# Shared experts of a mixture-of-experts layer on one core: from token-stationary tiles with transposes to weight-stationary chunks over two tiles

## The reference

```python
xn = _layernorm(x)
s  = attention(xn)                 # 16 query heads of 128, 4 key/value heads, rotary, causal
def ffn(x):                        # x: 2048 x 256
    scores = softmax(x @ gate_w.T) # 16 experts, the best 2 per token
    y  = sum over the token's 2 experts e of weight_e * (silu(x @ Wg_e) * (x @ Wu_e)) @ Wd_e    # 176 hidden
    gu = x @ shared_gate_up        # 256 x 704: gate 352 columns, up 352 columns
    y += (silu(gu[:, :352]) * gu[:, 352:]) @ shared_down                                       # 352 x 256
out = x + s * silu(ffn(xn))
```

## Time and profile before

| what | us |
|---|---|
| median of 3 runs | 671.38 |
| the profiled execution, whole | 671.35 |
| its span (first to last instruction) | 669.5 |
| busy: PE, DVE, ACT, POOL | 641.6, 538.2, 469.5, 482.7 |

### The profile page before, as it was taken

How to read it: one execution, slowest core, us unless ns; L and a number is a source line. 1 busy time by engine, 2 the same in 40 slices (tenths; PEclk the granted TensorE clock), 3 DMA queues, 4 the chain that set the end, 5 groups by cost and what they waited for, 6 DMA issues and landing times.

```text
span 669.5 us, 15670 instructions
## 1 busy us (share of the span) xinstructions
PE 641.6 (96%) x5108; PEld 462.9 (69%) x5171; DVE 538.2 (80%) x1621; ACT 469.5 (70%) x1271; POOL 482.7 (72%) x563
## 2 busy tenths in 40 slices
PE   7889999999999999999999999999999999999994
PEld 6656777767677677767677676767776777777772
DVE  4999999999999999999999999999974553333356
ACT  5799897868676676766686766767697745555542
POOL 4898979776667676788777878677769945555545
PEclk9999999999999999999999999999999999999998
DMA  8980001112500000000010101000144716667764
GB/s 287 347 260 1 2 9 25 24 11 41 155 1 1 1 1 2 1 33 27 25 40 8 40 8 40 25 17 1 51 68 139 196 26 145 139 143 137 223 248 164
DMA packets 70832, 52.11 MB, mean 78 GB/s; under 512 B 41392, under 2 KB 64144, under 8 KB 70768
## 3 DMA queue, kind: packets, MB, share of 16 engines
q1 hardware_dynamic: 66432, 40.57, 23.2%
q0 software_dynamic: 3792, 10.43, 5.1%
q10 hardware_dynamic: 544, 0.28, 0.2%
HBM read 24.75 MB, written 18.77 MB: 65 GB/s over the span
## 4 chain that ended last, share of the span: by engine, by line
PE 71%; DVE 12%; ACT 8%; issue 5%; DMA 2%; POOL 1%; SPq 0%; DVEq 0%; ACTq 0%
PE bank L1654 12%; PE bank L1592 12%; PE bank L1671 10%; PE bank L1623 9%; PE bank L1801 9%; PE bank L1638 8%; PE bank L1835 6%; PE bank L1810 2%; PE bank L1607 2%; DVE arena L1318 2%; ACT arena L956 2%; DVE arena L1291 2%; DVE arena L1290 1%; ACT arena L970 1%; ACT arena L964 1%
## 5 line engine op out<-in xcount | busy, mean ns | idle before, releaser
L956 ACT ACTIVATE arena<-bank,nmax 128x448 f32<-128x448 f32 (+7 forms) x256 | 125.8, 507 | 34.6 <-DVE nmax L1306 34.2
L655 POOL TENSOR_TENSOR arena<-arena,rinv 128x64 f32<-128x64 f32 (+2 forms) x192 | 102.2, 561 | 64.4 <-DVE rinv L1312 64.1
L970 ACT CAST arena<-bank 128x512 f16<-128x512 f32 (+1 forms) x192 | 94.5, 524 | 41.9 <-PE bank L1638 41.0
L1592 PE MATMUL bank<-xnT_both,arena 128*128 128x512 f16 (+2 forms) x435 | 114.3, 379 | 6.6 <-DVE xnT_both L1208 1.6
L1306 DVE CUSTOM_DVE_ANT_0 bank<-bank,mask_b 128x448 f32<-128x448 f32 (+7 forms) x256 | 109.5, 485 | 6.9 <-issue 6.9
L1654 PE MATMUL bank<-arena 128*128 128x512 f16 (+7 forms) x751 | 113.9, 297 | 1.1 <-DVE arena L1323 0.2
L1318 DVE TENSOR_TENSOR arena<-bank,arena 128x512 bf16<-128x512 f32 (+1 forms) x192 | 108.8, 594 | 4.3 <-ACT arena L970 3.7
L643 POOL TENSOR_TENSOR arena<-arena 128x512 f32<-128x512 f32 x79 | 100.8, 1276 | 11.6 <-DVE s_sb L1334 8.5
L1623 PE MATMUL bank<-arena 128*128 128x448 bf16 (+3 forms) x767 | 104.6, 286 | 2.2 <-POOL arena L648 1.2
L648 POOL TENSOR_TENSOR arena<-arena 128x512 bf16<-128x512 f32 x80 | 92.5, 1165 | 16.8 <-ACT arena L944 16.7
L1638 PE MATMUL bank<-ident_f,arena 128*128 128x128 f32 x640 | 94.0, 275 | 3.5 <-DVE arena L1318 2.5
(11 more groups left out here) (166 smaller groups left out, 1096.0 us busy)
## 6 DMA issues: line engine op xcount, KB each, us to landing
stage<-w_gate_up SPq DMA_DIRECT2D x16, 352.0 KB
xs_dram<-compare SPq DMA_DIRECT2D x3, 1560.0 KB, 16.1
arena<-ys_dram SPq DMA_DIRECT2D x8, 512.0 KB, 8.3
stage<-w_down SPq DMA_DIRECT2D x16, 176.0 KB
stage<-wq SPq DMA_DIRECT2D x4, 512.0 KB, 9.4
stage<-wo SPq DMA_DIRECT2D x4, 512.0 KB, 8.6
stage<-x SPq DMA_DIRECT2D x1, 2048.0 KB
out<-s_sb SPq DMA_DIRECT2D x7, 256.0 KB, 2.1
```

The costliest lines, as they stand in the source:

```text
L655: ins = pool.tensor_tensor(pr, pr, rinv[:, par, qt:qt + 1].to_broadcast([P, n]), ALU.mult)
L956: ins = act.activation(probs[par][:, P_AT[qt]:P_AT[qt] + n], score_bank[u][:, col:col + n], ACT.Exp, scale=-1.0, bias=nmax[:, par, qt:qt + ...
L970: act.copy(pT[j % 2][0][:, at:at + cols], pt_bank[(3 * j + u) % 2][:, 0:cols]).then_inc(pt_hi, 1)
L1592: ins = pe.matmul(ps[:], w[a][:, c * chunk:c * chunk + DH], tokens[m][:, c * TOK:c * TOK + S], start=(c == 0 and n == 0), stop=(c == KC - ...
```

## The change

The shared experts are computed the other way round. The weights are now the stationary operand (128 hidden columns, a chunk; the third chunk has 96), and the transposed tokens of two tiles (256 columns) move past them. The result stands with hidden columns on the partitions and needs no transpose. A step covers one chunk of gate and up for two tiles, so a pair of tiles takes 3 steps and there are 24 shared steps in place of 32: 15 ahead of the routed tiles and 9 behind them. ScalarE makes the high half from `hid` in SBUF, and VectorE makes the low half from `hid` and that high half, both in SBUF. The expert conversions on ScalarE stand in steps 0, 1, 2, 3, 5, 6, 7, 8, 10 in place of 0, 1, 3, 5, 6, 8, 10, 11, 13. The finished shared results leave PSUM for two tiles at once. The tables of the last groups are moved. `vector_hi`, which could give a high half to VectorE, returns False everywhere. The routed steps compute as before.

```diff
-END_SUMS = {-5: 0, -4: 1, 0: 2, 1: 3}
-END_PRODUCTS = {-3: 0, -2: 1}
-END_GATES = {-4: 0, -3: 1, 1: 2}
+END_SUMS = {-3: 0, -2: 1, 0: 2, 1: 3}
+END_PRODUCTS = {-1: 0, 0: 1}
+END_GATES = {-2: 0, -1: 1, 1: 2}
...
-        HI_STEPS = [5 * n // 3 for n in range(E_ROUTED - AHEAD)]
+        HI_STEPS = [5 * n // 4 for n in range(E_ROUTED - AHEAD)]
...
# ScalarE, a step
-                    act.activation(sg[:, st.ring(2), :], gu_bank[st.ring(2)][:, 0:INTER], ACT.Silu).then_inc(silued, 1)
-                if st.t:
-                    act.wait_ge(hT_ps, st.layers(1))
-                    for rows_, to, at in hidden_parts(st):
-                        ins = act.copy(hT_flat[0][rows_, to], hT_bank[st.parity(1)][rows_, at])
-                    ins.then_inc(hT_hi, 1)
+                    gate_ps, up_ps, to = silu_parts(st)
+                    act.activation(to, gate_ps, ACT.Silu).then_inc(silued, 1)
+                if st.t and st.routed(1):
+                    act.wait_ge(hT_ps, st.tile(1) + 1)
+                    act.copy(hidden_split(st)[0], hT_bank[st.parity(1)][0:HC, 0:2 * P]).then_inc(hT_hi, 1)
+                elif st.t and not vector_hi(st.like - 1):
+                    act.wait_ge(hidden, st.done(1))
+                    act.copy(hidden_split(st)[0], hidden_of(st, 1)).then_inc(hT_hi, 1)
...
# VectorE, a step
-                    dve.tensor_tensor(hid[...], gu_bank[st.ring(2)][:, INTER:GU], sg[:, st.ring(2), :], ALU.mult).then_inc(hidden, 1)
+                    gate_ps, up_ps, silu = silu_parts(st)
+                    dve.tensor_tensor(hidden_of(st, 0), up_ps, silu, ALU.mult).then_inc(hidden, 1)
                 if st.t:
-                    dve.wait_ge(hT_hi, st.layers(1))
-                    for rows_, to, at in hidden_parts(st):
-                        ins = dve.tensor_tensor(hT_flat[1][rows_, to], hT_bank[st.parity(1)][rows_, at], hT_flat[0][rows_, to], ALU.subtract)
-                    ins.then_inc(hT_lo, 1)
+                    hi, lo = hidden_split(st)
+                    dve.wait_ge(hT_hi, st.done(1))
+                    dve.tensor_tensor(lo, hT_bank[st.parity(1)][0:HC, 0:2 * P] if st.routed(1) else hidden_of(st, 1), hi, ALU.subtract).then_inc(hT_lo, 1)
...
-                    dve.tensor_copy(y_sb[:, d * D:(d + 1) * D], y_bank[st.parity(LAG)][:, 0:D]).then_inc(y_done, 1)
+                    dve.tensor_copy(y_sb[:, d * PAIR * D:(d + 1) * PAIR * D], y_bank[st.parity(LAG)][:, 0:PAIR * D]).then_inc(y_done, 1)
...
# TensorE, a shared step
+                        rows_, t = SHARED_ROWS[st.chunk()], st.pair() * PAIR * P
+                        for side in range(2):
+                            for c in range(KC):
+                                at = c * 2 * SHARED_I + side * SHARED_I + st.chunk() * P
+                                for p, (a, b) in enumerate(PASSES):
+                                    ins = pe.matmul(gu[0:rows_, side * PAIR * P:(side + 1) * PAIR * P], shared_s[b][:, at:at + rows_],
+                                                    xnT[a][:, c * TOK + t:c * TOK + t + PAIR * P],
+                                                    start=(side == 0 and c == 0 and p == 0), stop=(side == 1 and c == KC - 1 and p == 2))
...
+                    for p, (a, b) in enumerate(PASSES):
+                        if p == 2:
+                            pe.wait_ge(hT_lo, st.done(LAG))
+                        for t in range(PAIR):
+                            y = late_cols(pair * PAIR + t) if late else y_bank[st.parity(LAG)][:, t * D:(t + 1) * D]
+                            own = t == 0 or pair == PAIRS - 1
+                            ins = pe.matmul(y, hT_flat[a][0:rows_, at + t * P:at + (t + 1) * P], shared_s[b][0:rows_, down:down + D],
+                                            start=(chunk == 0 and p == 0 and own), stop=(chunk == CHUNKS - 1 and p == 2 and t == PAIR - 1 and not late))
```

More of the change, by code:

```diff
@@ L186, in projects, with done @@
     def projects(self, back):
[L187 to L198, removed]
+        return 0 <= self.like - back < STEPS
+    def done(self, back=0):
+        return self.n - back + 1
     def routed(self, back=0):
@@ L203, in tile, with shared, pair, chunk @@
     def tile(self, back=0):
[L204 to L208, removed]
+        return self.n - (back + SH_FIRST)
+    def shared(self, back=0):
         m = self.like - back
-        return m + SKIP if m >= ROUTED_END else m
-    def pair(self, back):
-        return self.place(back) % 4 - (E_SHARED - 1)
+        return m if m < SH_FIRST else m - R_TILES
+    def pair(self, back=0):
+        return self.shared(back) // CHUNKS
+    def chunk(self, back=0):
+        return self.shared(back) % CHUNKS
+    def parity(self, back):
+        return (self.tile(back) + PAIRS_FIRST) % 2 if self.routed(back) else self.pair(back) % 2
     def ring(self, of, back=0):
-        return (self.like - back) % of
+        return (self.like - back - SH_FIRST) % of
 def ffn_steps(step):
@@ L558, in _ @@
             sp.wait_ge(w_lo, len(WEIGHTS_ORDER))
[L559 to L564, removed]
+            for c in range(KC):
+                at = SHARED_AT + c * 2 * SHARED_I
+                sp.dma_start(stage[:, at:at + 2 * SHARED_I], shared_gu[c * P:(c + 1) * P, :]).then_inc(shared_in, 16)
             full, at = len(SHARED_ROWS) - 1, SHARED_AT + SHARED_WG
@@ L1794, in step @@
                         pe.wait_ge(xs_in[st.ring(4)], (st.tile() - st.ring(4)) * 4 + 16)
-                        tokens, chunk = xT[st.ring(4)], P
-                    else:
-                        tokens, chunk = [w[:, st.tile() * P:TOK + (st.tile() + 1) * P] for w in xnT], TOK
-                    w, half = weights(st), 0 if st.routed() else st.place() % E_SHARED
-                    for c in range(KC):
-                        for p, (a, b) in enumerate(PASSES):
-                            ins = pe.matmul(gu, tokens[a][:, c * chunk:c * chunk + P], w[b][:, half * WG + c * GU:half * WG + (c + 1) * GU],
-                                            start=(c == 0 and p == 0), stop=(c == KC - 1 and p == 2))
@@ L1803, in step @@
[L1803 to L1811 removed]
+                        w = weights(st)
@@ L1825, in step @@
-                    late = st.like - LAG >= ROUTED_END
-                    joins = late and st.tile(LAG) % BACK > 0 and st.tile(LAG) < NT - 1
-                    y = late_cols(st.tile(LAG)) if late else y_bank[st.parity(LAG)][:, 0:D]
-                    at = (st.ring(4, LAG) if st.routed(LAG) else st.pair(LAG)) * 2 * P
-                    chunks, down = ((HC, HC), WG) if st.routed(LAG) else (SHARED_ROWS, SHARED_WG)
-                    pe.wait_ge(hT_hi, st.layers(LAG))
+                    y, at = y_bank[st.parity(LAG)][:, 0:D], st.ring(4, LAG) * PAIR * P
```

130 lines of the change are left out of this document (76 added, 54 removed).

## The result

The changed kernel takes 678.77 us (median of 6 runs, 676.84 to 680.5), the kernel before 671.62 in the same session (6 runs, 671.11 to 672.2). The ratio is 1.0106, 95% interval 1.0086 to 1.0126: slower by 7.2 us, where 671.3 was predicted. The profiled execution took 680.5 us, the slowest of the six, so about 1.7 us of what follows is that execution's own.

The account below looks back on a forecast made before the run. TensorE's own work bounded the shared stretches, with GpSimd only 3.2 us ahead at the routed start. From 671.35, -0.9 there and +0.8 at the end gave 671.25, with 0.03 to the median 671.3 us; range 669.1 to 673.3.

Parts of the forecast that it names:

- The failed step: First shared stretch: low halves wait 0.7 on average behind GpSimd, exceeding slack in a quarter of 15 steps; 1 us, costing nothing.
- the 0.56 of register work: Ahead of the first routed product: 0.56 us added to TensorE's end of the first shared stretch, 543.1, giving 543.7.
- TensorE's own work: Shared steps: 0.11 us a matmul of 256 columns, 0.15 gained a tile; first stretch ends at 543.1 at the earliest.
- The hold on GpSimd: First shared stretch: each low half delays GpSimd's run by 0.2 us, about 13 times, so it ends at 545.0.
- GpSimd, not TensorE, now sets the routed start: Routed start: at 545.2, behind GpSimd's low halves, against 546.12 before, a gain of 0.9 us.
- rival 1: Faster: low halves do not hold GpSimd, TensorE sets the routed start, the end gains 0.4; 669.1 us, chance 0.20.
- ScalarE: First shared stretch: silu, high half and expert conversion take 1.94 us against a step of 1.98, so it fits.
- rival 4: ScalarE falls behind: an expert not landed holds the silu and TensorE; routed start 546.3, total 672.4 us, chance 0.06.
- The end: After the late projections: longer chain, last low half about 4.7 us behind the last projection; +0.8 us.
- The routed stage: Between the shared stretches: costed at nothing, shifting with the routed start; a length change over 0.5 from 90.6 refutes it.
- Rival 2: Slower: each low half holds GpSimd for its whole 0.43; routed start 548.2, total 674.3 us, chance 0.12.

Follow-up runs that it names:

- the first experiment: Changed kernel with the product with up of all shared steps kept in idle PSUM banks, giving low halves one PSUM input: 668.77 us against 671.54, ratio 0.9957.
- the memsets: Changed kernel with GpSimd's subtractions for experts 7 to 15 replaced by two memsets each, leaving out their low halves: 669.26 us against 670.92, ratio 0.9969.
- the extra instructions in the old kernel: Kernel before plus ten useless 128x256 VectorE subtractions of two SBUF tensors: 668.3 us, ratio 1.0012; control with one PSUM input: 667.4, ratio 0.9999.
- the kernel with one pause: Changed kernel with GpSimd waiting once, before expert 7, for the first low half: 674.12 us, ratio 1.0079.

## Why the prediction was wrong

**The failed step** is "A low half that meets GpSimd waits for the rest of an instruction of 1.54 or 1.18 us, on average 0.7", with its sum of 1 us and "It costs nothing". The wait was priced as if VectorE came next at the following end. It need not: it lost the turn at 6 of 13 ends, three of them in a row. One such row cost TensorE 4.14 us and 2.4 of clock, the others 1.43 and 0.64. In place of 1 us stood 8.6. TensorE was to be ready at 544.7 and was at 551.65: 7.6 more of waits and clock, less the 0.56 of register work, which did not appear. The rows at hand had it in the other direction: the 3.11 of L893 behind three L1474 in the earlier trace rows is an instruction of GpSimd that waited through several of VectorE's. It was read as a price of 0.61 each and not as a lost turn.

**TensorE's own work** was right: 0.11 a matmul of 256 columns (0.66 for 6), and 543.1 as its end without waits. In the first experiment TensorE works without a gap and the routed start is 542.79.

**The hold on GpSimd** was right in size: single subtractions beside a low half took 1.35 and 1.69 us in place of 1.16 and 1.52, so 0.17 to 0.2. It was wrong in number: seven such holds, 1.3 us in all and not 2.6, because the low halves queued up or fell into GpSimd's idle time. (The sum of all 22 subtractions grew by only 0.8, since the unhindered ones were 0.02 to 0.03 us shorter than the means in the earlier trace rows.) The Trainium skill ("SBUF — State Buffer", section "Who interferes with whom") states the exclusion for a whole instruction; the 0.2 is under half of the low half's duration of 0.41, of which no run shows how much keeps GpSimd off, and the 4.89 us of one low half is far above what blocking until the first finishes would give. The same section says that a GpSimd instruction that only writes is not in the way, and the 413 ns beside the memsets agree.

**"GpSimd, not TensorE, now sets the routed start"** was wrong in the changed kernel, where GpSimd ended at 548.03 and TensorE arrived at 551.65. It is wrong too where the collision is taken away: there GpSimd ends at 542.25, and TensorE works without a gap until 542.79. That is what rival 1 said, and its 669.1 us is close to the 668.77 of that kernel. Only with the conversions in their old steps did GpSimd come last (548.37).

**ScalarE** was priced as keeping up. It does by itself (even run of GpSimd in the first experiment), but it hands TensorE's stall on to GpSimd: 4.6 us idle, a chain like that of rival 4, with another origin: there it was to be a load that came late.

**The end** was right in its chain and in the last low half (4.9 behind the last projection, 4.7 predicted). Its price was +0.8, the profile has +1.7, and three other kernels that keep SBUF inputs there have +1.1 to +1.25 (32.3 to 32.5 us for 31.25). The kernels with PSUM inputs there spread from 30.4 to 32.25, so how much of it is the collision's is open.

**The routed stage** grew by 1.9 in the profiled execution, beyond the 0.5 allowed. In the seven experiments with the new form that keep all the work and did not run on the chip where the kernel before takes 667.40 us, it is 87.4 to 88.9, against 87.30 before. So a part of it is that execution's own; what the rest is, stays open.

**The rivals.** Rival 2 gave 674.3 with a condition on the hold (0.27 a low half) that was not met; the side was right, the mechanism another, and 4.5 us of the loss lie beyond it. No rival had a loss of turns, or a fall of the clock. What decides who gets in when GpSimd's next instruction stands ready is open: the longest waits were 4.89, 4.90 and 4.91 us in three kernels, 3.41 with the conversions moved, and 1.95 for the extra instructions in the old kernel. The arrival alone does not decide it: in those first four kernels the first low half started 0.54 or 0.55 us before the end of a GpSimd instruction of 88x512, and lost three turns in three of them and two in the fourth.

## What to carry to other kernels

Before an instruction of VectorE with two SBUF inputs is put on the path of TensorE, look at what GpSimd does in the same stretch: if it reads SBUF back to back, price the wait at several of its instructions and not at the rest of one. Keep one operand in PSUM if a bank is free, or give GpSimd's run a gap where the low half is due. A stall of TensorE is to be priced with the clock behind it (2.4 us behind the one of 4.14, nothing behind the one of 2.66) and with the engines whose queues stand behind its results.

## What was not expected of the hardware

- A ready VectorE instruction of 0.41 us took 4.89, past three ends of GpSimd instructions; it was repeated at 4.90 and 4.91 in two other kernels. Where it was given the first turn, a later one took 4.60.
- After 4.14 us without work in a busy stream the granted clock fell to about half (0.52, the level of 1.2 GHz in place of 2.4) and the next steps lost 2.4 us; after 3.21 us in the kernel with one pause it fell to 0.50 as well, and after 2.66 us in the kernel with the old conversion steps it stayed at 1.00. Filling the stall with matmuls of no use kept it at 1.00.
- The 0.56 us of "issue" ahead of the first routed product is not there in the changed kernel or in the first experiment, where the routed product follows the last shared one by 0.18 and 0.11 us. What it was is open.
